# Expert stage of a graph layer: VectorE's second block written out with its gate moved behind its products, GpSimd's wait for the updated rows moved to the first addition

## What is computed

```python
def _moe(x, router_w, w_gate, w_up, w_down):          # E = 8 experts, K = 2, D = 512, H = 1024
    logits = flat @ router_w.T
    topk_vals, topk_idx = jax.lax.top_k(logits, K)
    topk_w = jax.nn.softmax(topk_vals, axis=-1)
    ...
    y = jnp.einsum('esh,ehd->esd', jax.nn.silu(g) * u, w_down)
    out = jnp.einsum('esd,se->sd', y, dense_w)

x = x + gnn(layernorm(x)) + attention(layernorm(x))
x = x + moe(layernorm(x))
```

## Time and profile before

| | |
|---|---|
| time, median of 3 runs | 1526.06 us (1523.52 to 1564.74) |
| span of the profiled execution | 1527.5 us |
| PE busy over the span | 1374.7 us (90%) |
| DVE busy | 994.3 us (65%) |
| POOL busy | 739.8 us (48%) |
| ACT busy | 627.7 us (41%) |
| TensorE's mean granted clock | 0.948 of full |

### The profile page before, as it was taken

How to read it: one execution, slowest core, us unless ns; L and a number is a source line. 1 busy time by engine, 2 the same in 40 slices (tenths; PEclk the granted TensorE clock), 3 DMA queues, 4 the chain that set the end, 5 groups by cost and what they waited for, 6 DMA issues and landing times.

```text
span 1527.5 us, 24709 instructions
## 1 busy us (share of the span) xinstructions
PE 1374.7 (90%) x6836; PEld 656.2 (43%) x6837; DVE 994.3 (65%) x2484; ACT 627.7 (41%) x1094; POOL 739.8 (48%) x763
## 2 busy tenths in 40 slices
PE   6656998877869999999999999894899999999997
PEld 4343444434534444444444444483333334433333
DVE  7945666657737777777777777754545655556554
ACT  4454555545425666666666666561011111110110
POOL 3777777777766555555556555204322112211111
PEclk7787999989979999999999999996999999999999
DMA  5665333333249888888878888572333552514513
GB/s 190 221 208 159 118 113 116 112 115 110 99 141 292 248 248 249 251 247 249 250 237 260 249 249 248 182 258 51 73 95 121 183 172 47 192 41 165 193 28 93
DMA packets 125875, 262.52 MB, mean 172 GB/s; under 512 B 21073, under 2 KB 64808, under 8 KB 125147
## 3 DMA queue, kind: packets, MB, share of 16 engines
q0 software_dynamic: 48416, 141.37, 31.3%
q1 hardware_dynamic: 77410, 120.57, 23.5%
HBM read 204.35 MB, written 63.66 MB: 175 GB/s over the span
## 4 chain that ended last, share of the span: by engine, by line
PE 62%; POOL 20%; issue 8%; DMA 5%; DVE 3%; SPq 2%; ACT 0%; POOLq 0%; DVEq 0%; ACTq 0%
POOL edge_list L445 19%; PE psum L1320 19%; PE psum L1794 16%; PE psum L1806 8%; PE psum L1333 7%; PE psum L1328 5%; PE psum L1315 2%; DMA xrow<-in_x 1%; PE psum L1500 1%; SPq L1703 1%; DMA out_sums<-xrow 1%; SPq L368 1%; DMA out_x<-out_sums 1%; PE psum L1801 1%; DMA edge_list<-rec,place 1%
## 5 line engine op out<-in xcount | busy, mean ns | idle before, releaser
L1211 POOL DMA_INDIRECT shared<-node_table,shared x328 | 310.0, 945 | 212.4 <-DVE msg L1288 126.0
L445 POOL DMA_INDIRECT edge_list<-rec,place x313 | 317.2, 1014 | 101.3 <-issue 94.5
L1290 DVE TENSOR_TENSOR msg<-shared,psum 128x768 f32<-128x768 f32 x328 | 310.5, 947 | 0.0
L1320 PE MATMUL psum<-wf,hT 128*128 128x512 f32 x656 | 305.3, 608 | 3.0 <-ACT psum L1245 2.3
L1794 PE MATMUL psum<-shared,zT 128*64 128x512 f32 (+1 forms) x960 | 295.4, 596 | 1.6 <-DVE zT L1912 1.5
L1245 ACT COPY psum<-bias 128x512 f32<-128x512 f32 x328 | 193.3, 590 | 211.5 <-DVE msg L1290 194.8
L1288 DVE TENSOR_TENSOR msg<-shared,psum 128x256 f32<-128x256 f32 x328 | 136.2, 415 | 138.2 <-PE psum L1320 119.9
L1794 PEld LDWEIGHTS psum<-shared,zT 128*64 128x64 f32 (+1 forms) x960 | 114.4, 159 | 180.3 <-issue 178.4
L1320 PEld LDWEIGHTS psum<-wf,hT 128*128 128x128 f32 x656 | 118.2, 190 | 155.2 <-issue 136.5
L1806 PE MATMUL psum<-shared,hidT 128*64 128x512 f32 (+1 forms) x480 | 155.4, 602 | 6.3 <-DVE hidT L1933 6.3
L1755 POOL DMA_DIRECT2D ids<-slot_list x20 | 11.7, 582 | 294.7 <-DVE zN L1881 267.0
(11 more groups left out here) (338 smaller groups left out, 1563.9 us busy)
## 6 DMA issues: line engine op xcount, KB each, us to landing
shared<-edge_list SPq DMA_DIRECT2D x332, 130.0 KB
shared<-in_L_ffn_w_gate SPq DMA_DIRECT2D x8, 2048.0 KB, 9.1
shared<-in_L_ffn_w_up SPq DMA_DIRECT2D x8, 2048.0 KB, 14.7
shared<-in_L_ffn_w_down SPq DMA_DIRECT2D x8, 2048.0 KB, 19.5
shared<-node_table,shared POOLq DMA_INDIRECT x328
edge_list<-rec,place POOLq DMA_INDIRECT x313, 2.6
raw<-in_records SPq DMA_DIRECT2D x19, 256.0 KB, 3.4
xrow<-in_x SPq DMA_DIRECT2D x10, 250.0 KB
```

The costliest lines, as they stand in the source:

```text
L445: nc.gpsimd.indirect_dma_start(out=edge_list, out_offset=bass.IndirectOffsetOnAxis(ap=place[:n_, c:c + 1].bitcast(U32), axis=0), in_=rec[: ...
L1211: nc.gpsimd.indirect_dma_start(out=gat[:, k % G, :], out_offset=None, in_=table, in_offset=bass.IndirectOffsetOnAxis(ap=ix, axis=0)).then_ ...
L1290: nc.vector.tensor_tensor(m[:, 1:7, :].rearrange("p (a i) f -> p a i f", a=2), g[:, P:D].rearrange("p (i f) -> p i f", i=3).unsqueeze(1).t ...
L1320: nc.tensor.matmul(WP[k % TS][:], hT[:, (k // TS) % 2, (k % TS) * P:(k % TS + 1) * P], wf2[:], start=False, stop=True, skip_group_check=Tr ...
```

## The change

Three edits, all in the expert stage:

1. GpSimd no longer waits for `acc_in` ahead of its loop. The wait stands inside the loop, in front of `give(b)`, so it is met in every iteration.
2. VectorE's block 1 is written out ahead of the loop, as block 0 was. The loop runs from 2.
3. In block 1 alone, `gate(0)` stands behind the two products and the 16 transposes of `hidT`, ahead of the transposes of the next rows. From block 2 on the gate stands first, as before.

```diff
--- before.py
+++ after.py
@@ -1748,7 +1748,6 @@
                     gather(first_ids[:, 1:2])
                     enter(6, 2 * NC_)
                     pool.wait_ge(y_out, LISTED)
-                    pool.wait_ge(acc_in, 16 * NC_)
                     with pool.Fori(2, nb + 1) as b:
 
                         wait_alone(pool, turned, b + 1)
@@ -1758,6 +1757,7 @@
                         wait_alone(pool, ids_in, b * 16 - 16)
                         gather(ids[:, 0:1])
                         wait_alone(pool, to_in, b * 16 - 16)
+                        pool.wait_ge(acc_in, 16 * NC_)
                         give(b)
                     pool.dma_start(last_to[:], slot_list[bass.ds(nb * BLK - BLK, BLK), :]).then_inc(to_in, 16)
                     wait_alone(pool, to_in, nb * 16)
@@ -1917,8 +1917,8 @@
                         dve.wait_ge(to_in, b * 16 + 16)
                         nc.vector.tensor_scalar(yo[:], yraw[:], to[:, 1:2], None, ALU.mult).then_inc(gated, 1)
 
-                    def block_(b, last):
-                        if last is not None:
+                    def block_(b, last, first_given=False):
+                        if last is not None and not first_given:
                             gate(last)
                         dve.wait_ge(zt_done, b + 1)
                         for h_ in range(2):
@@ -1935,11 +1935,14 @@
                                 ins.then_inc(first_turned, 1)
                             else:
                                 ins.then_inc(hid_done, 1)
+                        if first_given:
+                            gate(last)
                         turn(b * 16 + 32)
                         copy_turned(b + 3)
 
                     block_(0, None)
-                    with dve.Fori(1, nb) as b:
+                    block_(1, 0, first_given=True)
+                    with dve.Fori(2, nb) as b:
                         block_(b, b - 1)
                     dve.wait_ge(last_in, 16)
                     dve.wait_ge(y_mm, nb)
```

## The result

| | before | after |
|---|---|---|
| median, 7 runs each | 1526.06 us (1519.4 to 1564.74) | 1516.93 us (1514.48 to 1520.81) |
| ratio, 95% interval | | 0.9948 (0.9934 to 0.9963) |
| profiled span | 1527.5 us | 1512.8 us |

A forecast was written before the change was run, and what follows sets the result against it. TensorE's work was taken to bound the expert stage, except for a hole in block 1. Its 6.30 of waiting and 2.78 of slower work make 9.08, less 0.05 is 9.0: 1526.06 - 9.0 = 1517.0 us, range 1513.5 to 1522.

The forecast's parts named there:

- The hole and its cause: Block 1: TensorE waits 6.30 us because VectorE's gate, waiting for the late `to`, stands ahead of the product; 9.08 with slower work.
- The half clock as part of the hole: TensorE behind block 1's wait: 2.78 us of slower work at clock 0.50, expected to go with the hole.
- my sum: Expert stage: 9.08 less 0.05 for GpSimd's added waits gives 9.0 us gained, the tail moving as a whole.
- the clock does not come back: Rival, block 1: half clock comes even without the hole, so only 6.30 us is gained, 1519.8; chance 0.04.
- 0.77 for the gate: VectorE, block 1: with the moved gate taking 0.40 us, TensorE's input for block 2 is still ready 0.77 early.
- 0.96 for the product: VectorE, block 1: product no longer behind the gate, so transposed hidden rows come 0.96 us ahead of TensorE's need.
- The 3.7 us for the gathered rows: GpSimd, block 1: with the wait moved, block 2's rows land at 1094.3, 3.7 us ahead of their transposes at 1098.00.
- my upper bound: GpSimd's loads beside the stores: at 5.6 us for `ids`, rows come by 1097.2, still in time, cost 0.
- the one on `ids`: Sign in the changed profile: GpSimd's first `ids` load stands near 5 us after block 1's begin, not 11.
- The first rival: Scatters seen complete only when stores end at 1092.97; TensorE waits 1.5 before block 2; gain 7.6 or 4.8; chance 0.14.
- The median: Whole kernel: 9.0 us taken off the median 1526.06 gives 1517.0 us, 0.6% faster.
- The low end of the range: Whole kernel: range 1513.5 to 1522, from 4.8 to 9.1 gained, with 2.5 of play below and 0.7 above.

The follow-up runs named there:

- e1: Changed kernel with GpSimd's wait for the stored rows put back ahead of its loop; ratio 0.9966 to the kernel before.
- e2: Kernel before with only GpSimd's wait moved to its addition, VectorE's gate still first in block 1; ratio 0.9965 to the kernel before.
- e3: Kernel before with VectorE's block 1 written out ahead of the loop, its gate still in front; ratio 1.0000 to the kernel before.
- e4 to e6: Changed kernel with 7, 12 and 16 constant-tile copies on VectorE in block 1 ahead of the transposes; block 1 took 23.81, 27.81 and 30.82 us.
- e10: Changed kernel with 18 unread matmuls ahead of block 0 and SyncE's last four stores held until GpSimd's scatters landed; ratio 0.9945 to the kernel before.
- e9: The changed kernel itself, measured again on another chip; ratio 0.9946 to the kernel before on that chip.

## Why the prediction was right

**The hole and its cause** held: 9.08 forecast for block 1, 9.19 measured, of 9.34 in the stage. e1 and e2 show that each edit shortens the hole by itself, e3 that writing out alone does nothing.

**The half clock as part of the hole** held: the 2.78 went with it, and e4 to e6 show that it hangs on the wait. That term is less firm than my sum made it look. Behind waits of 4.6 to 8.3 us the same kind of work cost between 1.94 and 2.89. The rival "the clock does not come back" is out.

**The margins.** 0.77 for the gate was 0.70, 0.96 for the product held. The 3.7 us for the gathered rows was mis-sized in two terms: the scatters' signal came at 7.14 after the block's begin and not by 4.0, and `ids` took 2.6 and not 2.0. Of the 3.1 in the first term, 0.8 is a misreading. The prediction says that no row shows the last scatter's landing, and takes 1087.0 from the empty queue; the DMA view of before from 1082 to 1084 has it, 6.5 after the issue, at 1087.81. The other 2.3 is a size that I took from one execution as if it were fixed: the same scatter took 8.7 in the changed kernel. Even my upper bound was passed: 1097.2 is 14.2 after the block's begin, and the rows came at 14.97. Its 5.6 is a median over all 20 scatters, also those ahead of the stores; beside the stores it is 6.4 and 5.9 in two stretches of before. That the cost was 0 all the same is in part luck: the rows were there 0.04 ahead of the 15.01 at which they were wanted, and 0.70 more of delay would have been hidden. Of the signs that the prediction names, the one on `ids` was not there: it left at 8.11 and not near 5.

**The first rival** (rows held until the stores are done) had the right direction and the wrong size. The stores do delay the landing, by some 5 us of its 8.7 as e10 shows, but it comes some 3 us before their end: it is at 1084.66, and their queue has packets until just ahead of 1088. It would have begun to hold TensorE with rows 0.7 us later than they were. e1, in which GpSimd does wait for the stores, cost 1.0, against the 1.5 of the rival's sum.

**The median.** I took the 9.0 off the median of three runs, 1526.06, for 1517.0; it came out at 1516.93. That this fits to 0.1 is luck: single executions of the same kernel lie over 6 us apart, and the ratio says 7.9 with 2.3 to either side. The low end of the range has a slip: 9.1 gained and 2.5 of play below give 1514.5, not 1513.5. And the row of one load of instructions is not all of them around the change; the DMA view of before from 1040 to 1140 has three such packets.

## What to carry to other kernels

Where an engine's program runs ahead of a late input, put the work that doesn't need it first, and do it only where the input is late: the same order in all blocks made the stage 12 us longer. Price a hole in TensorE's work as more than its width: behind waits of 4.6 to 8.3 us it cost 1.9 to 2.9 more here, behind 2.3 only 0.3. When a change starts small DMAs earlier, look at what else is moving then: beside 2.5 MB of stores the same scatters took two to three times as long to land. And look for the landing itself before you infer it from a queue that falls silent.

## What I had not expected of the hardware

The experiments' chips ran the same kernel 10% slower than the first measurement did; the chip of that one is not on record. In e9's profile the edge loop (L1211) goes from 536.0 to 1116.3, in the changed kernel's first profile from 447.7 to 964.2. In slices of 1/40 of the span the profile's page shows some 222 GB/s against 250 in that loop. The expert stage is the same to 1 us: 474.36 against 473.32 from table to end. The cause stays open; it is why I read the stage and not the totals.
